# A second staging buffer for the attention weights, and the first head pair's loads issued ahead of V's end

## The reference

```python
xn = layernorm(x)
qkv = xn @ W_attn + b_attn                 # W_attn [1024, 3072] f32
att = (q @ k.T) / sqrt(64) / temperature   # 16 heads of 64
att = softmax(att + slope[h] * (k_pos - q_pos), causal)
y   = (att @ v) @ W_proj + b_proj
h   = silu(xn @ wg.T) * (xn @ wu.T)        # int32 weights, times 1/127, hidden 3072
out = x + y + h @ wd.T
```

## Time and profile before

| | before |
|---|---|
| median of three runs | 2240.29 us |
| the profiled execution | 2240.16 us |
| its span, slowest core (core 5) | 2238.5 us |
| spans of all cores | 2217.2 to 2238.5 us |
| TensorE busy (matmul) | 1342.9 us, 60% |
| VectorE busy | 947.7 us, 42% |
| ScalarE busy | 899.9 us, 40% |
| GpSimd busy | 78.6 us, 4% |
| DMA, mean over the span | 89 GB/s |
| stages 1 and 2 (to the first load of `wattn`) | 0 to 848.7 us |
| stage 3 | 848.7 to 1098.2 us |
| stage 4 (from the first score matmul) | 1121.8 to 2238.5 us |

### The profile page before, as it was taken

The page is one execution under the profiler, slowest core; times in us unless marked ns, Lnnn a source line. Parts: engine busy times, 40 slices in busy tenths (PEclk is TensorE's granted clock), DMA queues, the critical chain, the costliest instruction groups (busy, mean ns, idle before and its releaser), DMA issues.

```text
span 2238.5 us, 25575 instructions; the slowest of 8 cores (2217.2 to 2238.5 us)
## 1 busy us (share of the span) xinstructions
PE 1342.9 (60%) x8642; PEld 708.0 (32%) x8642; DVE 947.7 (42%) x1601; ACT 899.9 (40%) x1521; POOL 78.6 (4%) x148
## 2 busy tenths in 40 slices
PE   0001099898989970699655454645454564656666
PEld 0001044343434430244233333333333333333333
DVE  2335210110101101341077675858586775745553
ACT  3335332130311300001166676757576666643332
POOL 0010000000000000131000000000000000000000
PEclk9855599999999995799855555555555555566767
DMA  7787443341533315221200001010101001022212
GB/s 253 250 286 234 145 156 113 124 157 59 169 105 123 130 40 194 98 76 36 85 10 25 33 1 57 1 57 1 57 1 57 1 19 39 1 85 76 75 42 82
DMA packets 46185, 198.84 MB, mean 89 GB/s; under 512 B 6119, under 2 KB 6120, under 8 KB 38378
## 3 DMA queue, kind: packets, MB, share of 16 engines
q1 hardware_dynamic: 31978, 148.96, 20.3%
q0 software_dynamic: 14080, 48.24, 5.8%
HBM read 157.34 MB, written 39.85 MB: 88 GB/s over the span
## 4 chain that ended last, share of the span: by engine, by line
PE 50%; DMA 18%; ACT 12%; DVE 10%; issue 8%; SPq 0%; DVEq 0%; ACTq 0%; POOL 0%; POOLq 0%
PE ps_tr L763 9%; PE ps_dn L404 8%; PE ps_g L360 7%; PE ps_u L368 7%; ACT ptb L727 6%; PE ps_qk L483 5%; DVE snegp L651 5%; ACT pbuf L687 4%; PE ps_tr L858 4%; PE ps_y L788 3%; DMA abcp<-alibi_bc 3%; PE ps_v L516 3%; DMA wst<-wattn 2%; PE ps_s L632 2%; DMA wg_sc<-cbuf 2%
## 5 line engine op out<-in xcount | busy, mean ns | idle before, releaser
L651 DVE SCALAR_TENSOR_TENSOR snegp<-ps_s,abcp 128x1024 f32<-128x1024 f32 (+2 forms) x320 | 330.5, 1058 | 345.7 <-PE ps_s L638 345.6
L727 ACT ACTIVATE ptb<-ps_tr 128x1024 bf16<-128x1024 f32 (+7 forms) x416 | 295.8, 727 | 412.4 <-PE ps_tr L763 410.8
L763 PE MATMUL ps_tr<-ident_s,pbuf 128*128 128x128 bf16 x2176 | 277.2, 295 | 299.6 <-ACT ptb L727 204.1
L613 DVE TENSOR_REDUCE ncmx<-snegp 128x2 f32<-128x1024 f32 (+2 forms) x320 | 328.4, 1052 | 3.5
L763 PEld LDWEIGHTS ps_tr<-ident_s,pbuf 128*128 128x128 bf16 x2176 | 196.3, 131 | 397.4 <-issue 395.4
L687 ACT ACTIVATE pbuf<-snegp,negmax 128x128 bf16<-128x128 f32 (+15 forms) x256 | 304.5, 1193 | 18.4 <-DVE negmax L668 17.6
L632 PE MATMUL ps_s<-k_hp,q_hp 64*128 64x512 bf16 (+2 forms) x320 | 141.1, 501 | 176.1 <-DVE snegp L651 94.7
L404 PE MATMUL ps_dn<-wdres,hbuf 128*128 128x512 bf16 x768 | 177.6, 392 | 37.9 <-DVE xfout L425 32.4
L360 PE MATMUL ps_g<-xnT,wgbuf 128*128 128x512 bf16 x768 | 183.1, 382 | 9.6 <-DMA wubuf<-wu_sc 9.6
L368 PE MATMUL ps_u<-xnT,wubuf 128*128 128x512 bf16 x768 | 182.5, 381 | 0.0
L294 PE MATMUL ps<-ident_s,xn_st 128*128 128x128 bf16 x128 | 16.1, 303 | 259.8 <-DVE xn_st L277 259.8
(11 more groups left out here) (65 smaller groups left out, 1050.3 us busy)
## 6 DMA issues: line engine op xcount, KB each, us to landing
wgbuf<-wg_sc SPq DMA_DIRECT2D x48, 512.0 KB
wubuf<-wu_sc SPq DMA_DIRECT2D x48, 512.0 KB
abcp<-alibi_bc SPq DMA_DIRECT2D x16, 1024.0 KB
wistage<-wg_r SPq DMA_DIRECT2D x12, 1024.0 KB
wistage<-wu_r SPq DMA_DIRECT2D x12, 1024.0 KB
wistage<-wd_r SPq DMA_DIRECT2D x12, 1024.0 KB
wst<-wattn SPq DMA_DIRECT2D x8, 1536.0 KB
xstage<-xin SPq DMA_DIRECT2D x16, 512.0 KB
```

Source lines behind the costliest of these rows:

```text
L613: cd = S.op("vector", lambda e, par=par, c0=c0, w=w, ci=ci: e.tensor_reduce(ncmx[:, par * 8:par * 8 + 8].rearrange("p (j c) -> p j c", j=2 ...
L651: stt = S.op("vector", lambda e, par=par, hb=hp % 2, aoff=aoff, c0=c0, w=w, rA=rA: e.scalar_tensor_tensor(snegp[par].rearrange("p (j t) -> ...
L727: return e.activation(dst, src, AF.Copy)
L763: lasttr = S.op("tensor", lambda e, par=par, j=j, kc=kc, slot=slot, idx=idx, n=len(kcs): e.matmul(ps_tr[:, slot * 512 + (kc % 4) * 128: sl ...
```

## The change

- `wst3` becomes two buffers, used in turn. A load waits for the cast of the load two before it. The order in SBUF is changed: `qkst` now lies ahead of the staging buffers.
- `abcp0`, `q_hp` and `k_hp` are given out last in stage 4, behind `outsb`, so that of stage 3 they overlap only the staging buffers of `wattn`.
- The first head pair's four loads are written out ahead of the loads of `wpj_b`. The ALiBi loads wait for the last weight cast and for the last stores of `qkst` buffers 2 and 3 (the last two stores of k); the q load waits for the last cast and for the last two stores of row blocks 0 of q and of k. They no longer wait for V. The loads of `wpj_b` keep their waits and follow behind.
- No arithmetic, no size and no other wait is changed.

```diff
-                wst3 = E3(nc.sbuf_tensor("wst3", [128, 3 * C], F32, side="right"))
                 qkst = [...]
+                wst3 = [E3(nc.sbuf_tensor(f"wst3_{i}", [128, 3 * C], F32, side="right")) for i in range(2)]
...
                 for dc in range(DC):
-                    ld = S.dma("sync", lambda e, dc=dc: e.dma_start(
-                        out=wst3[:, :], in_=wattn[dc * 128:(dc + 1) * 128, :]),
-                        waits=[("v", wst_war), ("pe", p2_pe), ("v", p2_v), ("a", p2_a)]
-                              + p2_xf_st)
+                    wb = dc % 2
+                    ld = S.dma("sync", lambda e, dc=dc, wb=wb: e.dma_start(
+                        out=wst3[wb][:, :], in_=wattn[dc * 128:(dc + 1) * 128, :]),
+                        waits=[("v", wst_war[wb])]
+                              + ([("pe", p2_pe), ("v", p2_v), ("a", p2_a)] + p2_xf_st
+                                 if dc < 2 else []))
...
-            def emit_group_load(hp):
+            def emit_group_load(hp, early=False):
                 hb = hp % 2
-                wts = [("v", abc_war[0])]
-                if hp == 0:
-                    wts += [("pe", p3_pe), ("v", p3_v), ("a", p3_a)] + qk_st_fin
+                if early:
+                    wts = [wat_fin, qk_st_war[2], qk_st_war[3]]
+                    wq = [wat_fin] + store_of_fc[0] + store_of_fc[8]
+                else:
+                    wts = [("v", abc_war[0])]
+                    if hp == 0:
+                        wts += [("pe", p3_pe), ("v", p3_v), ("a", p3_a)] + qk_st_fin
+                    wq = [("pe", qk_war[hb])] if qk_war[hb] else []
...
             outsb = E4b(nc.sbuf_tensor("outsb", [128, C], F32, side="right"))
+            q_hp = [...]
+            k_hp = [...]
+            abcp0 = E4b(nc.sbuf_tensor("abcp0", [128, 2 * T], F32, side="right"))
+            abcp = [abcp0, abcp0]
+            wat_fin = ("v", wat_cv)
+            emit_group_load(0, early=(T >= 2048))
...
-                    if qt == 0:
+                    if qt == 0 and hp > 0:
                         emit_group_load(hp)
```

More of the change, by code:

```diff
@@ L462, in build_program @@
                 wat_cv = 0
-                wst_war = 0
+                wst_war = [0, 0]
                 for dc in range(DC):
-                    ld = S.dma("sync", lambda e, dc=dc: e.dma_start(
-                        out=wst3[:, :], in_=wattn[dc * 128:(dc + 1) * 128, :]),
-                        waits=[("v", wst_war), ("pe", p2_pe), ("v", p2_v), ("a", p2_a)]
-                              + p2_xf_st)
-                    wat_cv = S.op("vector", lambda e, dc=dc: e.tensor_copy(
-                        wattn_b[:, dc * 3072:(dc + 1) * 3072], wst3[:, :]),
+                    wb = dc % 2
[4 more added lines that the diff above has]
+                                 if dc < 2 else []))
+                    wat_cv = S.op("vector", lambda e, dc=dc, wb=wb: e.tensor_copy(
+                        wattn_b[:, dc * 3072:(dc + 1) * 3072], wst3[wb][:, :]),
                         waits=[ld], inc="v")
-                    wst_war = wat_cv
+                    wst_war[wb] = wat_cv
                 qk_rel = [("a", ce), ("v", 0), ("v", 0), ("v", 0)]
                 qk_st_war = [("v", 0)] * 4
+                store_of_fc = {}
                 qk_st_fin = None
@@ L508, in build_program @@
                         qk_st_war[bank] = sto
+                        store_of_fc.setdefault(fc, []).append(sto)
+                        store_of_fc[fc] = store_of_fc[fc][-2:]
                         qk_rel[bank] = ("v", ev)
@@ L543, in build_program @@
             ptb2 = [E4b(nc.sbuf_tensor(f"ptb2_{i}", [128, 1024], BF16, side="right")) for i in range(8)]
[L544 to L547, removed]
             ncmx = E4b(nc.sbuf_tensor("ncmx", [128, 24], F32, side="right"))
@@ L591, in emit_group_load @@
                     out=abcp0[:, T:2 * T], in_=alibi_bc[2 * hp + 1, :, :]))
-                wq = [("pe", qk_war[hb])] if qk_war[hb] else []
                 l3 = S.dma("sync", lambda e, hp=hp, hb=hb: e.dma_start(
@@ L816, in build_program @@
             outsb = E4b(nc.sbuf_tensor("outsb", [128, C], F32, side="right"))
+            q_hp = [E4b(nc.sbuf_tensor(f"q_hp{i}", [128, T], BF16, side="right")) for i in range(2)]
+            k_hp = [E4b(nc.sbuf_tensor(f"k_hp{i}", [128, T], BF16, side="right")) for i in range(2)]
+            abcp0 = E4b(nc.sbuf_tensor("abcp0", [128, 2 * T], F32, side="right"))
+            abcp = [abcp0, abcp0]
+            wat_fin = ("v", wat_cv)
+            emit_group_load(0, early=(T >= 2048))
             pj_rel = [0]
```

## The result

The changed kernel takes 2191.15 us, the median of ten runs (2185.3 to 2255.0); against the kernel before on the same chip the ratio is 0.978, 95% interval 0.975 to 0.982. A second series on one chip gave 2195.2 us and 0.977 (0.973 to 0.981). So it is faster, by 2.2 to 2.3%; whether by more than 2% is left open, as the intervals reach back to 1.8 and 1.95%. (In some executions of either kernel the cores of one die run slower: the median of all ten runs of before, 2258.95 us, holds several of these, the ratios leave them out, and of a profile with such a die only the other die's cores are read.)

The account below looks back on a forecast made before the run. The prediction took TensorE's two waits for transfers, 66.3 us before the projections and 24.3 us before the scores, as the bound; savings of 24.2 + 23.4 = 47.6 us from 2240.2 gave 2192.6 us, range 2185 to 2200.

Parts of the forecast that it names:

- What bounds the two stretches: TensorE waits 66.3 us before the first q/k projection matmul (weight cast) and 24.3 us before the first score (k load).
- Part one: Weight loads before the projections: two staging buffers cut the stretch from 66.85 to 42.6 us, saving 24.2.
- The sum's term 8 x 4.77 us: Weight stretch: eight loads of 1.573 MB at 330 GB/s, 4.77 us each.
- the end given for 306 GB/s: Weight stretch at the middle of the crowded rows' rates: 45.5 us, saving 21.3.
- casts over 5.2 us apart: Weight stretch: the sign that would show the crowd; 4.2 to 5.1 us apart would show the forecast right.
- the crowd: Rival on the weight loads: other cores' streaming takes part of the gain, leaving it within 2%; 2198.4 us at 286 GB/s; chance 0.25.
- The floor of a buffer's round: Weight loads: load, cast and handovers take 8.4 us, so two buffers give at least 4.2 us a load.
- Part two: Before the first score: the first group load goes out early under V's matmuls; wait 0.9 us for 24.3, saving 23.4.
- The clock: Rival in the projections: a shorter rest costs TensorE its 2.4 GHz; half the stretch at 1.2 gives 2284 us; chance 0.02.
- the 0 to 1.4 us allowed for: First 10 us of scores: possible gain from starting at 2.4 GHz without the idle gap; counted as nothing in the sum.
- The border of 2%: Whole kernel: 2195.5 us, 44.8 us below before, separates faster from no change; faster got 0.68.
- Core 5 ends last: Whole kernel: core 5, first wait 66.3 us against core 7's 70.4, should still set the end.

Follow-up runs that it names:

- half the bytes: The changed kernel, two buffers, each load bringing 1536 of 3072 columns and the cast taking them twice; weight stretch 31.3 us on average, no kernel time given.
- order-only run: The changed kernel with the first head pair's loads ahead of the projection weights but waiting for V's end: 2205.9 us, ratio 0.984.

## Why the prediction was right, and where it was wrong

*What bounds the two stretches*: right. The two waits of the earlier trace rows were the whole price; the stretches between and behind them kept their length (112.4 and 68.5 us; attention 1113.8 and 1113.6).

*Part one, the size*: this is the step that failed. The sum's term 8 x 4.77 us took one rate, 330 GB/s, for all loads of all cores, with the DMA engines busy above 0.9, and gave a stretch of 42.6 us and 24.2 saved. On core 5 the step between casts was 5.36 us, the share 0.79 and the stretch 47.6 us; it saved 19.2, less than the end given for 306 GB/s (21.3). By the prediction's own sign, casts over 5.2 us apart, this was the crowd, a rival with a chance of 0.25. The mean of the cores, 4.97 us or 316 GB/s, lies between the 330 taken and the crowd's 306. With three buffers the runs show two rates in place of the one: 3.70 us a load while the neighbour is idle, about 5.2 beside it. Cores 4 and 5 of the profiled execution began their loads at 841.79 and 841.78, so they ran side by side all the way, 46.6 and 47.6 us; on the other cores it was 42.1 to 44.9. The neighbour is not all of it. The seven pairs of the other executions that began within 2.6 us of each other had 44.1 to 45.6 us on average and got 593 to 617 GB/s together while both loaded; cores 4 and 5 here got 571 (282 and 289 from 849.9 to 886.4 us, share 0.84). Two buffers also leave holes: the third brought the mean step from 4.97 to 4.49 us with the same bytes. Why cores 4 and 5 got still less stays open. The floor of a buffer's round, with the ends of a load (2.4 us) in it, holds up: half the bytes ran into it.

*Why the time came out all the same*: in the profiled execution the miss of 5 us was made up by stages 1 and 2, 7 us shorter on core 5. On the mean of the cores part one saved 24.7 us, as forecast, but from 68.9 to 44.2 where the forecast went from 66.85 to 42.6: both ends were longer than forecast, by 2.0 and 1.6 us, and these misses nearly cancel. So part of the agreement is luck.

*Part two*: right, 23.4 forecast, 24.0 on core 5. Nothing held the early loads (1005.55, after the last k store), V covered them, and the 9.3 us of projection weights hide beside the scores. The order-only run shows that the cover and the order each carry half.

*The clock*: no loss in the projections. The first scores begin at 0.63 in place of 0.50. On core 5 the first head pair takes 102.5 us (1071.57 to 1174.02) where it took 103.5, but on the mean of the cores 103.0 where it took 103.1. So of the 0 to 1.4 us allowed for, next to nothing came, and taking nothing was right.

*The border of 2%*: the two ratios lie just beyond it and their intervals on both sides of it, so the runs don't settle whether the kernel is faster by over 2%, to which the prediction gave 0.68.

*Core 5 ends last*: it did in the profiled execution, but only in 3 of the 12 executions of the first series whose cores are on record. In the profile of the second series core 7 did, which began the weight loads 20 us after core 5; there the order was set before the change's stretch.

## What to carry to other kernels

A second buffer takes away the wait for the consumer, and what is left is about the larger of two numbers: the buffer's round divided by the buffers, and the bytes over the rate that the core gets while its neighbour does the same. Take the second from a row in which the neighbour streams too, and expect it to change within the stretch. Here the two were 4.2 and 5.2 us a load and the mean step of the changed kernel 4.97; a third buffer, which lowers the first, brought it to 4.49. A load that is needed next should stand ahead of a load that is needed later, and be issued under the last stretch that leaves the queues idle; the same question, asked at each later pair start, was worth more here than the first answer.

## What the runs showed of the hardware

With three loads in flight, two neighbouring cores that loaded at once got about 304 GB/s each, 608 together, and one of them alone 425. The change between the two is seen within one load of the neighbour's start or end. With two loads in flight, eight pairs side by side got 571 to 617 together. A wait that is taken off one source can come back from another: of the 38.4 us that VectorE waited for loads on core 6, 27.6 came back as waits for scores.
